# A transformer layer on eight cores: an x block loaded on demand at the joint of two sequences, and the last layer norm's preparation moved to ScalarE

## The reference

```python
# --- attention ---
q, k, v = x @ kernel[0], x @ kernel[1], x @ kernel[2]      # per head
scores = einsum('bhsd,bhtd->bhst', q, k) * 1/(64*64*16)
out = einsum('bhst,bhtd->bhsd', softmax(scores), v)
x = layernorm(x + out.reshape(b, s, 1024) @ WO[0])
# --- feed forward with token mix ---
x_prev = x shifted by one token (zeros first)
xr = mu_r * x + (1 - mu_r) * x_prev
xk = mu_k * x + (1 - mu_k) * x_prev
r = sigmoid(xr @ W_r.T)
out = r * (square(relu(xk @ W_k.T)) @ W_v.T)
x = layernorm(x + out)
```

## Time and profile before

| | us |
|---|---|
| median of 2 runs | 2547.0 |
| the two runs | 2513.86, 2580.14 |
| the profiled run, device time | 2520.56 |
| its span on the slowest core (core 7) | 2518.9 |
| spans of the other cores | 2498.0 to 2517.0 |

### The profile page before, as it was taken

The page is one execution under the profiler, slowest core; times in us unless marked ns, Lnnn a source line. Parts: engine busy times, 40 slices in busy tenths (PEclk is TensorE's granted clock), DMA queues, the critical chain, the costliest instruction groups (busy, mean ns, idle before and its releaser), DMA issues.

```text
span 2518.9 us, 30106 instructions; the slowest of 8 cores (2498.0 to 2518.9 us)
## 1 busy us (share of the span) xinstructions
PE 2102.4 (83%) x10176; PEld 709.8 (28%) x10176; DVE 827.6 (33%) x1361; ACT 1251.0 (50%) x1449; POOL 20.1 (1%) x27
## 2 busy tenths in 40 slices
PE   0999889788888988897898888978988898889745
PEld 0442222232322232232342222322232232223212
DVE  0330004223341524043550140432434152504356
ACT  0017755756375646653006556575637564764420
POOL 0000000000000000000000000000000000000000
PEclk9998889899989997898999898989997898989867
DMA  9349600023101410131220131102220132012201
GB/s 185 50 77 209 167 1 34 1 68 84 68 1 34 117 67 1 34 116 68 34 59 25 36 115 34 34 1 68 84 68 1 34 118 67 1 33 82 85 12 58
DMA packets 83056, 153.04 MB, mean 61 GB/s; under 512 B 1952, under 2 KB 16352, under 8 KB 82912
## 3 DMA queue, kind: packets, MB, share of 16 engines
q1 hardware_dynamic: 51184, 102.87, 12.2%
q0 software_dynamic: 23024, 31.47, 8.4%
q10 hardware_dynamic: 8704, 16.78, 1.9%
HBM read 151.12 MB, written 31.46 MB: 72 GB/s over the span
## 4 chain that ended last, share of the span: by engine, by line
PE 57%; ACT 21%; DVE 11%; issue 7%; another core or an unknown queue 2%; ACTq 1%; DMA 1%; DVEq 0%; SPq 0%
PE psg L99 29%; ACT pb L109 14%; PE pspv L99 11%; PE psden L99 10%; ACT lta L109 5%; PE psa L99 3%; PE psb L99 3%; DVE xka L118 2%; DVE rg L118 2%; DVE stv L118 2%; ACT rcr L109 1%; DVE recb L118 1%; DVE y L118 1%; DVE xra L118 1%
## 5 line engine op out<-in xcount | busy, mean ns | idle before, releaser
L109 ACT ACTIVATE pb<-psb 128x1024 bf16<-128x1024 f32 x512 | 523.9, 1023 | 386.2 <-PE psden L99 200.8
L109 ACT ACTIVATE pb<-psa 128x1024 bf16<-128x1024 f32 x512 | 523.0, 1022 | 117.9 <-PE psa L99 117.8
L99 PE MATMUL pspv<-pb,vtb 128*64 128x512 bf16 x2048 | 432.4, 430 | 20.5 <-DVE aba L118 20.2
L99 PE MATMUL psden<-pb,cstb 128*32 128x512 bf16 x2048 | 414.8, 414 | 0.0
L99 PE MATMUL psg<-xra,ws 128*128 128x512 bf16 x1352 | 354.9, 415 | 21.8 <-DVE qtb L118 11.7
L118 DVE TENSOR_TENSOR aba<-pspv,rsb 128x512 bf16<-128x512 f32 x64 | 44.2, 691 | 766.7 <-ACT rsb L109 765.6
L99 PE MATMUL psa<-qtb,ktb 64*128 64x512 bf16 x1024 | 215.2, 406 | 91.3 <-ACT pb L109 82.3
L99 PE MATMUL psb<-qtb,ktb 64*128 64x512 bf16 x1024 | 207.9, 400 | 62.2 <-ACT pb L109 62.2
L99 PEld LDWEIGHTS psg<-xra,ws 128*128 128x128 bf16 x1352 | 130.1, 104 | 220.9 <-issue 109.5
L99 PEld LDWEIGHTS pspv<-pb,vtb 128*64 128x64 bf16 x2048 | 111.0, 110 | 286.5 <-issue 286.5
L99 PEld LDWEIGHTS psden<-pb,cstb 128*32 128x32 bf16 x2048 | 93.9, 94 | 255.0 <-issue 255.0
(11 more groups left out here) (120 smaller groups left out, 1686.7 us busy)
## 6 DMA issues: line engine op xcount, KB each, us to landing
ws<-wsc SPq DMA_DIRECT2D x34, 2048.0 KB, 9.4
ws<-wts POOLq DMA_DIRECT2D x8, 2048.0 KB, 22.9
y<-xT SPq DMA_DIRECT2D x8, 2048.0 KB, 10.5
outT<-outb ACTq DMA_DIRECT2D x32, 512.0 KB, 4.6
wsc<-ws SPq DMA_DIRECT2D x7, 2048.0 KB, 15.0
xra<-xT POOLq DMA_DIRECT2D x7, 1024.0 KB, 10.1
rg<-xT POOLq DMA_DIRECT2D x4, 1024.0 KB, 8.6
aba<-xT POOLq DMA_DIRECT2D x3, 1024.0 KB, 8.9
```

The lines of the kernel that those rows point to most:

```text
L99: i = e.matmul(_o, _l, _r, start=_st, stop=_sp, tile_position=_tp, skip_group_check=True)
L109: i = e.activation(_o, _i, _f, scale=_s, bias=_b)
```

## The change

Three edits:

1. Block 1 of sequence 1 is no longer loaded into XRA at the end of sequence 0. `emit_kv` loads it itself into ABA, as it does in sequence 0: behind the last matmul that reads ABA in `emit_wo_pairs`. Block 3, which also goes to ABA, has to wait for block 1's V projection.
2. In the last `emit_wo_pairs` of all, the 8 casts and 8 squares are done on ScalarE (Copy and Square, both from OUTB), not on VectorE.
3. For the last block, LN1's apply pairs and the mix pairs alternate, where all apply pairs came first.

```diff
-                dsts = {1: ABA if seq == 0 else XRA, 2: RG, 3: ABA, 0: RG}
-                buf_free = {id(ABA): (c_g, xb_free[0]), id(RG): None,
-                            id(XRA): None}
+                dsts = {1: ABA, 2: RG, 3: ABA, 0: RG}
+                buf_free = {id(ABA): (c_g, xb_free[0]), id(RG): None}
...
-                if seq == 0:
-                    emit_load(1)
-                else:
-                    loads[1] = xra_nxb[0]
+                emit_load(1)
...
-            def emit_wo_pairs(u):
+            def emit_wo_pairs(u, casts_on_a=False):
...
                 u["yadds"] = nv
+                u["ycast_sem"] = c_va
+                if casts_on_a:
+                    wait("a", c_vg, c_vg.n)
+                    nva = 0
+                    for j in range(8):
+                        act(RG[:, j * QT:(j + 1) * QT],
+                            OUTB[:, j * QT:(j + 1) * QT], AF.Copy, inc=c_ar)
+                        nva = act(XKA[:, j * QT:(j + 1) * QT],
+                                  OUTB[:, j * QT:(j + 1) * QT], AF.Square,
+                                  inc=c_ar)
+                    u["ycast"] = nva
+                    u["ycast_sem"] = c_ar
+                    return
...
-                wait("t", c_va, u["ycast"])
+                wait("t", u.get("ycast_sem", c_va), u["ycast"])
...
-                if t < NT - 1 or seq + 1 < NSEQ:
-                    src_off = (seq * D * S + (t + 1) * QT if t < NT - 1
-                               else (seq + 1) * D * S + 1 * QT)
+                if t < NT - 1:
...
-        emit_wo_pairs(prev)
+        emit_wo_pairs(prev, casts_on_a=True)
...
-        emit_ln_bcast_apply(prev, Y1)
-        emit_mix(prev)
+        st_f = emit_ln_bcast_head(prev, Y1)
+        for op in range(0, 8, 2):
+            emit_ln_apply_pair(st_f, op)
+            emit_mix_pair(prev, op)
```

More of the change, by code:

```diff
@@ L339, in build_nc @@
         gkt = [0]
-        kv_nxb0 = [0]
-        xra_nxb = [0]
         xb_free = [0]
@@ L441, in build_nc @@
             kvf = []
+            kv_nxb0 = [0]
+            xra_nxb = [0]
             if prev is not None:
@@ L1021, in build_nc @@
                         bass.AP(XRA, 0, [[NCH * QT, 128], [QT, 8], [1, QT]]),
-                        bass.AP(xT, src_off,
+                        bass.AP(xT, seq * D * S + (t + 1) * QT,
                                 [[S, 128], [128 * S, 8], [1, QT]]), c_xb)
                 prev = u
-        emit_wo_pairs(prev)
+        emit_wo_pairs(prev, casts_on_a=True)
         last_ycast[0] = prev["yadds"]
```

## The result

| | before | after |
|---|---|---|
| median of all runs, us | 2512.86 (42 runs) | 2521.2 (43 runs) |
| profiled run, us | 2520.56 | 2521.73 |
| its span on the slowest core | 2518.9 | 2520.2 |

The ratio of after to before is 1.0033, with a 95% interval from 1.002 to 1.0047: the changed kernel is about 8.3 us slower (5.0 to 11.8), which is inside the 2% that count as no change. The median of before had been 2547.0 when only two runs were shown; over 42 runs it is 34 us lower.

The account below looks back on a forecast made before the run. The prediction took TensorE to bound the kernel through most of the span. Joint +6.0, tail casts and squares -0.9, interleaving 0 made +5.1 on 2520.56: 2526 us, range 2512 to 2586, called no change.

Parts of the forecast that it names:

- The joint: Between the two sequences, TensorE waits for V weights and x block together, 15.5 us in place of 9.5: +6.0 us.
- Rival (a): At the start of sequence 1, the x load hides under the weight load, adding nothing: 2520 us; chance 0.15.
- Rival (b): Between the sequences, loads run strictly one after the other, +9.0 us: 2529; with a 30.9 us load, 2541; chance 0.08.
- What follows the joint: In sequence 1 behind the later start, block loads, VectorE's layer norm work and the clock restart cost nothing more.
- Block 3's load: Sequence 1's load into ABA waits for block 1's V projection, 3.4 us more, with 29 us of cover: no cost.
- The restart after the pause: First matmuls of sequence 1 run at the lower clock level; a longer pause makes no longer restart: nothing.
- The tail: Behind the last WO projection, casts and squares on ScalarE take 8.6 us in place of 9.55; -0.9 us taken.
- rival (c): Square on ScalarE in the tail forces function table reloads: +2.6 us (2528) up to +20.5 (2546); chance 0.10.
- The wait for the mix: In the tail, TensorE's wait of 29 us stays with alternating apply and mix pairs: nothing, within 0.5 us.
- rival (d): Granted clock of the cores falls in sequence 1, from 0.90 to 0.84, stretching it: about 2572 us; chance 0.05.
- The sum: Whole kernel: +6.0 - 0.9 + 0 = +5.1 us on the profiled 2520.56: 2525.7, said as 2526.
- The upper end of 2586: Top of the range for the whole kernel: 2526 + 60, as the run at 2580.14 is 60 above the profiled one.

Follow-up runs that it names:

- edit 1 alone: x block 1 of sequence 1 loaded on demand into ABA, tail untouched, against the kernel before: ratio 1.0029, median 2521.15 against 2513.72 us.

## Why the prediction was right or wrong

**The joint: right in cause, close in size.** It said +6.0 from 15.5 us for both landings; the waits show +5.7. The DMA engine time of the two loads was forecast as 13.0 us and is 13.1. That a second load adds its engine time fits this number and the run with the x block loaded alone, where the added wait is gone; that each engine works on one packet at a time was an assumption, and no run shows it. Rival (a), the hidden load, is out: the wait rose on every core. The estimate by the formula of "DMA: Bandwidth & Descriptors" in the Trainium skill (section on the anatomy of one DMA, given there for loads issued from GpSimd), 9.2 us for both, would have been this rival; the x block took 13.9. Rival (b), the strict sequence, fits only the core with the longest wait (18.0 us); its 30.9 was not seen.

**What follows the joint: right.** Block 3's load was issued 1233.85 - 1201.64 = 32.2 us behind the first K matmul, 29.0 before: 3.2 later, 3.4 forecast, and no wait for it appears. The restart after the pause costs no more than 0.3 us: from the first K matmul to the first scores the means over the cores are 128.4 us before and 128.7 after.

**The tail: right up to the mix, too small behind it.** 8.66 us from the last add to the statistics (8.6 forecast), steps of 0.52 (0.52), one ACT_TABLE_LOAD in every kernel, so Square lies in the set that is loaded and rival (c) is out. The wait for the mix stayed at 29.2. What the prediction left out is the stretch behind the mix, which it took as unchanged: there the mean tail lost another 1.9 us, and the 8 matmuls behind the 3.22 us wait stood at the lower clock level on fewer cores. The gain of the tail is thus 2.3 us in the traces and not 0.95.

**The clock, rival (d): no sign.** The mean clock of the compared runs of after is 0.907. Before it was 0.909 in one call and 0.907 in two others, so what differs lies within what the kernel before does by itself.

**Where it was wrong: the time that the sum was added to, and with it the direction as it reads.** The sum, +5.1 us, is near what the traces show (+4.8 by the waits, +3.6 by the two places as a whole). But it was added to one profiled run of 2520.56 and set beside a median of two runs, 2547.0. So "2526" reads as 0.8% faster than the time shown, while the kernel is 0.33% slower. The prediction took the profiled run to be "near the lower" of the two and thus typical. It was not: it is 7.7 us above the median of 42 runs, and its slowest core had a clock of 0.898. Typical was the lower run, 2513.86, plus 5.1 = 2519, against 2521.2 measured. That 2519 comes so near is in part luck, for the sum was 3 us under the measured growth of 8.3. The step that failed is thus not an edit's price but the base, and what should have been said is the sign: one edit costs 6 us and the other two together gain 1 to 2, so slightly slower. The upper end of 2586, taken from the run at 2580.14, was far too wide for a median.

**What stays open.** The time grew by 8.3 us (5.0 to 11.8), the waits by 4.8, just under the interval, and the two places as a whole by 3.6; for edit 1 alone it is 7.3 us of time for 6.3 at the joint. The rest of the span can't settle it: the stretch from the start to the last WO matmul of sequence 0 has means of 1176.5 to 1182.3 us over the twelve profiled runs, and the one from the first scores of sequence 1 to the last add 1056.8 to 1062.6, so they move by as much as is missing. The mean span over the cores grew by 4.9 from before to after, across two calls, and by 7.6 for edit 1 alone, within one. The wait at the joint spreads over 3.4 us between cores after, and over 1.5 before, which would make the slowest core grow by more than the mean; that the spread is the cause was not shown.

## What to carry to other kernels

When a transfer is moved from early to on demand, ask what TensorE already waits for at that place, and add the DMA engine times of all loads that must have landed, not the longest. Here a prefetch was worth 6 us and not the 9 of its landing, and the order of two loads was worth as much. A wait placed ahead of a whole phase should stand ahead of the part that reads the data: moving one wait gained 6 us at the joint here. And a forecast is no better than the time that it is added to: two runs of this kernel lay 66 us apart, and their middle 34 us above the median of 42.

## What the runs showed of the hardware

An x load that casts f32 to bf16 and writes 1 MB took about as much engine time (6.3 to 7.1 us) as a plain load that writes 2 MB (5.6 to 6.8). Both read 2 MB and both are 1040 packets, so the engine time follows what is read and not what is written; whether it is bytes or packets that count was not told apart. The GB/s of the profile count what is written: read by it, a casting load seems half as fast as it is.

A pause of TensorE at the joint of 16, 27 and 53 us, where it stood for 10 us before, cost about its added length: 5 to 8, 16 and 39 to 45 us. A wait of 3.22 us in the tail was in some cores followed by 8 matmuls at a granted clock of 0.50 that took 3.57 us, and in others by the same at 1.00 in 1.89 us.
